# A fused two-layer graph kernel: order of TensorE's steps in the first edge stage, setup loads, scatter turns

## The reference

```python
# x: 100000 x 128 float32; src, dst: 25000 edges, dst sorted
# layer 0: messages of the edges, maximum over the edges of one dst
feat = concatenate([x[dst], x[src] - x[dst]], axis=-1)
messages = relu(feat @ W1 + b1) @ W2 + b2
x = layernorm(x + where(isneginf(segment_max(messages, dst)), 0, segment_max(messages, dst)))
# layer 1: sum over the edges, two products, residual product
h = x + segment_sum(x[src], dst)
h = maximum(h @ V1 + c1, 0) @ V2 + c2
out = layernorm(x + (x @ Wres + bres) + h)
```

## Time and profile before

| What | Value |
|---|---|
| Median of three runs | 1114.36 us |
| The profiled execution, its own time | 1113.68 us |
| Its span in the profile | 1111.9 us |
| PE busy | 1068.9 us (96%) |
| DVE busy | 934.9 us (84%) |
| ACT busy | 896.9 us (81%) |
| GpSimd busy | 765.8 us (69%) |
| Granted TensorE clock, mean | 0.995 |

### The profile page before, as it was taken

How to read it: one execution, slowest core, us unless ns; L and a number is a source line. 1 busy time by engine, 2 the same in 40 slices (tenths; PEclk the granted TensorE clock), 3 DMA queues, 4 the chain that set the end, 5 groups by cost and what they waited for, 6 DMA issues and landing times.

```text
span 1111.9 us, 27074 instructions
## 1 busy us (share of the span) xinstructions
PE 1068.9 (96%) x7463; PEld 835.6 (75%) x7463; DVE 934.9 (84%) x3645; ACT 896.9 (81%) x3888; POOL 765.8 (69%) x798
## 2 busy tenths in 40 slices
PE   5899999999999999999899999999999999999995
PEld 3677877777666666666578888888888878888884
DVE  7799888897888888888868787878787789999993
ACT  2887878787888888888897888888888887777774
POOL 6777777777777777772047777777777777777712
PEclk9999999999999999999999999999999999999998
DMA  5788877875888888877576667676756566666652
GB/s 151 214 244 247 230 244 231 246 233 152 220 222 232 248 232 221 233 223 214 164 232 198 213 191 215 190 214 191 214 166 194 172 202 217 218 217 220 218 171 86
DMA packets 172255, 231.86 MB, mean 209 GB/s; under 512 B 25658, under 2 KB 90791, under 8 KB 172106
## 3 DMA queue, kind: packets, MB, share of 16 engines
q1 hardware_dynamic: 145434, 180.66, 52.0%
q0 software_dynamic: 25088, 48.94, 17.3%
q10 hardware_dynamic: 1584, 0.53, 0.2%
HBM read 129.48 MB, written 102.78 MB: 209 GB/s over the span
## 4 chain that ended last, share of the span: by engine, by line
PE 65%; POOL 19%; issue 8%; DVE 4%; ACT 2%; DMA 1%; SPq 0%; POOLq 0%; DVEq 0%; ACTq 0%
POOL edge_rows L522 17%; PE psY L1125 10%; PE psY L1126 10%; PE psH L1137 10%; PE psE L1118 6%; PE psT L1118 5%; PE psE L1257 4%; PE psE L1126 4%; PE psE L1125 4%; PE psE L1293 4%; PE psE L1248 3%; PE psE L1242 3%; PE psE L1240 3%; POOL xd_early L522 1%; DVE shared L758 1%
## 5 line engine op out<-in xcount | busy, mean ns | idle before, releaser
L1125 PE MATMUL psY<-wc,hT 128*128 128x128 f32 x1568 | 304.1, 276 | 0.5 <-DVE o_rows L646 0.4
L1126 PE MATMUL psY<-wcr,xT 128*128 128x128 f32 x1568 | 303.9, 276 | 0.0
L522 POOL DMA_INDIRECT edge_rows<-x1e_table,idx x196 | 188.8, 963 | 118.5 <-issue 59.4
L526 POOL DMA_INDIRECT out<-edge_rows,idx x196 | 195.0, 995 | 100.0 <-issue 61.9
L1125 PEld LDWEIGHTS psY<-wc,hT 128*128 128x128 f32 x1568 | 240.7, 192 | 13.3 <-issue 13.3
L949 ACT ACTIVATE junk<-psY 128x128 f32<-128x128 f32 x784 | 209.3, 302 | 49.3 <-PE psY L1126 49.1
L1126 PEld LDWEIGHTS psY<-wcr,xT 128*128 128x128 f32 x1568 | 238.8, 193 | 0.0
L522 POOL DMA_INDIRECT edge_rows<-in_x,idx x196 | 189.8, 968 | 65.5 <-issue 59.4
L609 DVE TENSOR_SCALAR x<-x_in,mv,rs 128x128 f32<-128x128 f32 x784 | 221.7, 361 | 0.6
L1137 PE MATMUL psH<-xT,wc 128*128 128x512 f32 x392 | 204.5, 604 | 6.2 <-ACT xT L944 5.5
L1118 PEld LDWEIGHTS psT<-ident,x 128*128 128x128 f32 x784 | 99.2, 143 | 110.1 <-issue 104.1
(11 more groups left out here) (125 smaller groups left out, 1993.4 us busy)
## 6 DMA issues: line engine op xcount, KB each, us to landing
x_in<-in_x SPq DMA_DIRECT2D x196, 256.0 KB
out<-o_rows SPq DMA_DIRECT2D x195, 256.0 KB
src_bc<-src_dram SPq DMA_DIRECT2D x49, 256.0 KB, 4.5
mask<-mask_dram SPq DMA_DIRECT2D x98, 128.0 KB
x1eT_spill<-x1eT SPq DMA_DIRECT2D x49, 256.0 KB, 2.4
x1e_table<-edge_rows SPq DMA_DIRECT2D x49, 256.0 KB, 3.5
x1e_table<-shared SPq DMA_DIRECT2D x49, 256.0 KB, 3.8
x1eT<-x1eT_spill SPq DMA_DIRECT2D x49, 256.0 KB, 3.1
```

The costliest lines, as they stand in the source:

```text
L522: nc.gpsimd.indirect_dma_start(to, None, table, bass.IndirectOffsetOnAxis(idx[:, what, t:t + 1], 0)).then_inc(landed[n % FLIGHT], 16)
L526: nc.gpsimd.indirect_dma_start(table, bass.IndirectOffsetOnAxis(idx[:, SCAT, t:t + 1], 0), frm, None, bounds_check=limit, oob_is_err=False ...
L1125: t_.matmul(to[:, cut(t)], h[:, cut(t)], wc2[:, :], start=t == 0, stop=False, skip_group_check=True)
L1126: last = t_.matmul(to[:, cut(t)], xt[:, cut(t)], wcr[:, :], start=False, stop=t == TILES - 1, skip_group_check=True)
```

## The change

The change has these parts. In stage A, PE's `transposed(n)` moves from h = 1 to h = 0 and `first_product(n-1)` from h = 0 to h = 1; ACT's `copy_xT` and `relu` change places with them. The three whole dense steps that followed steps 49 to 51 are now inside those steps. On DVE, ACT and SP they are still the last thing of the step; on PE they stand ahead of `transpose_x1e`, `center_z` and `transpose_in`. In the setup SP issues x of unit 0 before the source indices, the biases have a semaphore of their own and are issued after the first root, DVE does norm 1 of unit 0 around the index cast, ACT copies the weights instead of DVE, and PE does the first product of unit 0 ahead of the last weight products. In the head `copy_xT` comes ahead of `root`. SP's first two `feed_s` move from behind the head to behind its unit 6. The last scatters get a count for each of the four `stored` semaphores, computed on DVE in `late_stores` when stage B begins.

```diff
@@ walk
             for s in range(GROUPS, STEPS):
-                step_a(s, None, 0)
-                dense(A_LAST + s - GROUPS)
+                step_a(s, A_LAST + s - GROUPS, A_STEPS)
@@ sync
+                if n == HEAD - 2:
+                    sp.wait_ge(s_srcst, 32)
+                    feed_s(0)
+                    feed_s(1)
             def lead_s():
-                sp.wait_ge(s_srcst, 32)
-                feed_s(0)
-                feed_s(1)
+                pass
@@ step_a, sync
                 load_mask(s + 1)
+                if h == A_STEPS:
+                    dense(n)
@@ sync, setup
+            load(0)
             sp.wait_ge(s_iz, 1)
             load_indices(0, src, s_is)
-            load(0)
             load(1)
@@ gpsimd
+            def late_needed(at):
+                return [pool.value_load(late_16[0:1, at, k:k + 1], min_val=0, max_val=16 * BODIES) for k in range(SLOTS)]
+            def await_stores(counts):
                 for k in range(SLOTS):
-                    pool.wait_ge(stored[k], count)
+                    pool.wait_ge(stored[k], counts[k])
                 pool.nop().then_inc(s_turn, 1)
+            pool.wait_ge(s_late, 4)
+            for g in range(LATE, WHOLE):
+                counts = late_needed(g - LATE)
+                pool.wait_ge(res_done, g + 1)
+                await_stores(counts)
+                for t in range(TILES):
+                    scatter_tile(g, t)
             for g in range(WHOLE, GROUPS):
                 pool.wait_ge(res_done, g + 1)
                 for t in range(TILES):
-                    await_stores(count if t < WHOLE_TILES else 16 * BODIES)
-                    if t + 1 < WHOLE_TILES:
-                        count = stores_needed(WHOLE + t + 1)
-                    scatter(out, edge_rows[:, cut(g * TILES + t)], g * TILES + t, scatter_number(g) + t)
+                    await_stores(late_needed(SLOTS + t) if t < WHOLE_TILES else [16 * BODIES] * SLOTS)
+                    scatter_tile(g, t)
@@ vector
+            def late_stores():
+                counts = late_16[:, :, :].rearrange("o n k -> o (n k)")
+                v.tensor_scalar(late_unit[:, :], last_dst[:, LATE:WHOLE + WHOLE_TILES], ROWS.bit_length() - 1, None,
+                                ALU.arith_shift_right).then_inc(s_late, 1)
+                dve.wait_ge(s_late, 1)
+                for k in range(SLOTS):
+                    last = v.tensor_scalar(late_16[:, :, k], late_unit[:, :], SLOTS - k, None, ALU.add)
+                last.then_inc(s_late, 1)
...
             def lead_b():
                 dve.wait_ge(eh_done, GROUPS)
+                late_stores()
@@ vector, setup
+            norm1_stats(0)
+            norm1_var(0)
             dve.wait_ge(s_is, 16 * 4)
             link(v.tensor_copy(idx_f[:, 0, :, :], idx_in[:, 0, :, :]))
-            norm1_stats(0)
-            norm1_var(0)
+            recip(-2)
+            norm1_scale(0)
             dve.wait_ge(s_pe, 1)
             link(v.tensor_copy(idx[:, 0, :], psE[0][:, 0:2 * P]))
@@ scalar
             def head(n):
-                if n == 0:
-                    copy_xT(0)
-                    root(0)
-                else:
-                    dense(n)
+                norm2_var(n - 3)
+                relu(n - 1)
+                copy_xT(n)
+                if n == 0:
+                    keep_weights()
+                root(n)
+                finish(n - 3)
@@ step_a, scalar
-                if n is not None:
+                if h == A_STEPS:
+                    dense(n)
+                elif n is not None:
                     if h == 0:
+                        copy_xT(n)
+                    if h == 1:
                         relu(n - 1)
-                    if h == 1:
-                        copy_xT(n)
@@ scalar, setup
             root(-2)
+            load_biases()
             root(-1)
-            act.wait_ge(s_w, 16 * 11)
+            act.wait_ge(s_b, 16 * 5)
@@ step_a, tensor
                 edge_product2(s - 1)
                 edge_product1(s)
-                if n is not None:
+                if h == A_STEPS:
+                    dense(n)
+                elif n is not None:
                     if h == 0:
+                        transposed(n)
+                    if h == 1:
                         first_product(n - 1)
-                    if h == 1:
-                        transposed(n)
                     if h >= 2:
                         second_half(n - 2, h - 2)
                 transpose_x1e(s - 2)
```

More of the change, by code:

```diff
@@ L554, in _, with stores_needed @@
                     gather(edge_rows[:, cut(g * TILES + t)], x1e_table, PLACE, g * TILES + t, z_number(g) + t)
[L556 to L561, removed]
+            def stores_needed(g):
+                top = g + SLOTS - 1
+                earlier = pool.value_load(stores_16[0:1, top:top + 1], min_val=0, max_val=16 * LAST)
+                return [pool.snap(earlier + 16)] * SLOTS
@@ L570, in _ @@
             pool.wait_ge(s_dv, SETUP_STEPS)
-            count = stores_needed(last_group_of(0))
-            for g in range(WHOLE):
+            counts = stores_needed(0)
+            for g in range(LATE):
                 pool.wait_ge(res_done, g + 1)
-                if g % SLOTS == 0 or g > LATE:
-                    await_stores(count)
+                if g % SLOTS == 0:
+                    await_stores(counts)
                 for t in range(TILES):
-                    if t == TILES - 1 and (g % SLOTS == SLOTS - 1 or g >= LATE):
-                        count = stores_needed(last_group_of(g + 1) if g + 1 < WHOLE else WHOLE)
-                    scatter(out, edge_rows[:, cut(g * TILES + t)], g * TILES + t, scatter_number(g) + t)
+                    if t == TILES - 1 and g % SLOTS == SLOTS - 1 and g + 1 < LATE:
+                        counts = stores_needed(g + 1)
+                    scatter_tile(g, t)
@@ L979, in dense @@
                 norm2_var(n - 3)
+                if n >= UNITS:
+                    root(n)
                 relu(n - 1)
-                root(n)
+                if n < UNITS:
+                    root(n)
                 copy_xT(n)
@@ L1174, in transpose_indices, with last_weights @@
                 last.then_inc(s_pe, 1)
+            def last_weights():
+                t_.matmul(psE[3][:, 0:P], wtmp[:, 1, :], center[:, :], start=True, stop=True)
+                t_.matmul(psE[1][:, 0:P], wtmp[:, 2, :], center[:, :], start=True, stop=True).then_inc(s_pe, 1)
             def head(n):
-                if n > 0:
+                if n == 1:
+                    pe.wait_ge(s_copied, 1)
+                    first_product(0)
+                    last_weights()
+                    transposed(1)
+                elif n > 1:
                     first_half(n)
@@ L1323, in _ @@
             t_.transpose(psE[2][:, 2 * P:3 * P], raw[:, W2R, :], ident[:, :]).then_inc(s_pe, 1)
-            pe.wait_ge(s_dv, SRC_IDX_STEP + 2)
-            t_.matmul(psE[3][:, 0:P], wtmp[:, 1, :], center[:, :], start=True, stop=True)
-            t_.matmul(psE[3][:, P:2 * P], wtmp[:, 2, :], center[:, :], start=True, stop=True).then_inc(s_pe, 1)
             walk(head, dense, lead_s, step_s, lead_a, step_a, lead_b, step_b)
```

61 lines of the change are left out of this document (39 added, 22 removed).

## The result

The changed kernel takes 1118.65 us (median of six runs), the kernel before 1114.58 beside it. The ratio is 1.0036, with a 95% interval of 1.0023 to 1.0049. So it is slower by 4.1 us; 1113.0 was forecast, in a range up to 1115.0. The profiled execution of the changed kernel took 1119.12 us with a span of 1117.3, so the two profiled spans lie 5.4 us apart, 1.3 more than the medians. What follows is read from them.

A forecast was written before the change was run, and what follows sets the result against it. PE, busy for 96% of the span, was taken as the bound, with ACT behind it from step 49. Terms -0.7 + 0 + 3.05 + 0.1 - 3.8 = -1.4 us gave 1113.0 us against the median, range 1110.0 to 1115.0.

The forecast's parts named there:

- First gather: Setup: with x of unit 0 issued earlier, the first gather starts at 8.5 in place of 9.27, 0.8 us early.
- the slower rival: Setup: index loads queue behind x, land at 8 us, first gather 1.9 us late; 1115.7 us in all, 9% chance.
- the chain of gathers runs at its own pace: After the first gather: gathers follow each other some 1.25 us apart, without a stop that matters.
- Stage S: Stage S to A: loads 3.3 us earlier gain PE some 3 us, gathers cap it; net gain 0.7 us.
- the landing moves only with the first gather: Start of stage A: the awaited gather's landing comes earlier only by the first gather's 0.8 us.
- the meeting at group 5: Start of stage A: gather chain and PE's chain arrive practically together at group 5, so a gain in one alone is lost.
- The exchange: Stage A: 0.43 us of PE work moved between intervals gains nothing; bounds 0.5 gained and 0.3 lost over twelve units.
- the 1.4 us of holes in a unit: Stage A: a unit of 23.52 us costs PE 22.15 us of work, the rest being holes, mostly ahead of h = 1 centring.
- The tail: Steps 49 to 51: centring gains 0.92 us, late edge transposes hold ACT, lower clock costs 1.4; loss 3.05 us.
- the 1.65 of the order: Step 50: unit 73 ahead of group 48's edge transposes makes ACT's copy of them start 1.65 us late.
- DVE's counts: Beginning of stage B: seven operations and three waits, about 0.9 us, hidden; cost 0 to 0.3, summed as 0.1.
- The end: Last scatters: finer turns start the last scatter about 0.25 us after the last landing; gain 3.8 us.

The follow-up runs named there:

- e4: The kernel before with only the finer scatter turns of the change: 1111.55 us, ratio 0.9976.
- e12: The kernel before with the source gathers of the last five groups moved behind later destination gathers, nothing else: 1112.60 us, ratio 0.9985.
- e1: The changed kernel with PE's whole dense units of steps 49 to 51 put back behind the edge work: 1114.41 us, ratio 0.9996.
- e3: The changed kernel with the stage A exchange of transposes and first product undone: 1118.36 us, ratio 1.0038.
- e6: The changed kernel with four extra unread products on PE in its wait for unit 72 in step 50: 1116.18 us, ratio 1.0014.
- e2: The changed kernel with the first two loads of source values issued behind the head again: 1115.75 us, ratio 1.0010.
- e5: The changed kernel with five extra unread first products on PE ahead of its wait for the gathers of group 4: 1115.92 us, ratio 1.0010.
- e9: The changed kernel with the last five groups' source gathers moved later and all three dense units behind the edge work on PE: 1106.02 us, ratio 0.9925.
- e10: The changed kernel with the last five groups' source gathers later, all dense units behind PE's edge work, first source loads behind the head: 1107.88 us, ratio 0.9942.

## Why the prediction was wrong

**First gather.** The mechanism was right (8.85, forecast 8.5; the index loads did come later behind x), the term was not. The old setup starts gathering at 9.27, 8.81 (e4) and 9.06 (e12), the new one at 8.57 to 9.10 in eleven executions, so on the mean the new one gains 0.2 us, not 0.8, with ranges that overlap. The index loads landed near 5.9 in place of 4.2, so the slower rival's order was seen, but only 1.7 us late. Moreover the last gather of group 4 was issued at 282.80 to 283.91 in all eight kernels with the old order of gathers, whatever the first one was. The step "the chain of gathers runs at its own pace" failed: most are 1.25 us apart, but 18 to 23 of the first 216 are 1.40 to 1.65, and in the changed kernel's trace five more of these than before outweighed the head start. This is a small part: e1, e3 and e6 issued that gather at 282.8 to 283.2, as before, and were 3.2 to 3.4 us late at step 5 all the same.

**Stage S.** It was right that the gathers cap PE's gain, and that PE would wait for `src_bc`. Three steps failed. PE's gain from the earlier loads was 1.2 us at step 1 (e2), not 3: DVE's wait went, but the rest of that stretch did not follow. The step "the landing moves only with the first gather" failed: an earlier PE brought SP's transfers ahead of the last gather of group 4, and it landed 4.7 us after its issue (283.91 to 288.60), when 3.7 had been enough in the trace of before and 2.5 was in e4. I had set the meeting at group 5 and left out group 4. And the price of the wait was taken as zero. I named the lowered clock for the tail and not here, where the same change made a wait of 5.5 us; e5 gives it as 2.0 to 2.7 us. Gain of 0.7 forecast, 4.1 lost in the profiled executions; against e4, which had PE early and a short wait, the loss at step 5 is 4.7. The 296.79 in that working, for the stalled centring before, is 296.69 in the row; it moves the gain by 0.1.

**The exchange.** Right, in mechanism and size: 23.54 us a unit, a new wait of 0.18 ahead of h = 0, e3 within 0.3 us. Only the 1.4 us of holes in a unit were too many: PE is busy for 22.75 of the 23.52 us from 367.24 to 390.76, and the wait of 0.75 is nearly the whole rest.

**The tail.** Right in mechanism and order: the centring at full clock, ACT's copy 0.9 early, the wait of 3.85 (forecast 3.9), the copy of group 48 late. Mis-sized was the clock: 1.4 us was read from a stretch in which only a part of the work ran at the lower level, while all of unit 73 did, 6.1 us in place of 3.1. e6 has the clock at 2.5 to 3.1 of the 4.2 to 4.9 us. The copy of group 48 was 4.65 us late, which is the 1.65 of the order and 3.0 of the slow unit, and with the clock kept up (e6) the tail is 1.8 us longer than before's. That bears the 1.65 out, though roughly: e6's tail is 0.5 us longer than e1's and 2.7 longer than e9's, with the same order on PE in both as before.

The stretch that the 1.4 us came from does not even repeat. The same waits of about 1.7 and 1.3 us left the centring of step 49 at 2.08, 1.76, 2.08 and 2.03 us in before, e1, e10 and e12, and at 1.16, full clock, in e4 and e9. So the 0.9 us to be gained by that centring were there in some executions only.

**DVE's counts.** No run takes them apart. e4 has them, and its tail is 27.9 us against 27.4 in before and 27.3 in e12, so they cost 0.5 at most by these traces; 0.1 was forecast.

**The end.** 3.8 forecast, 3.0 measured (e4). The reads of counts were not all of the 1.45 us behind the landing; 0.92 remain, where 0.25 was forecast. The 0.4 us of ACT's earlier root were no term of the forecast.

**The sum.** With the measured terms: +4.1 at the start of stage A, 0, +4.2 to 4.9 in the tail, -3.0 to -3.5 at the end, so 5.3 to 5.5, the distance of the two spans; the medians are 4.1 apart. Two terms had the wrong size by the same cause, a clock that falls in a long wait, and one of them, at the start of stage A, the wrong sign by that and by the late landing. The slower rival was another mechanism (indices late), so the 5% for slower did not cover the true one.

What stays open is why some gathers take 0.15 to 0.4 us longer, whether SP's transfers are what held the last gather of group 4 up, and why the kernel before in its profiled execution reached stage A 1.5 to 1.9 us later than e4 and e12, with the same order on PE.

## What to carry to other kernels

An engine that arrives earlier at a transfer which does not come earlier gains nothing, and on TensorE it can lose: its wait grows, the clock falls, and the work behind the wait runs at half speed. It can also release other transfers early, and in these traces the awaited one then landed later; so first move the transfer. Work put into a hole is only a gain if its own inputs are there: in an in-order queue, a unit that waits holds up all behind it, here the few transposes that the bound engine needed. Where a long wait can't be avoided, products that nobody reads keep the clock up (1.5 to 2.7 us each time here), and a meeting of two chains should be read from more than one execution.

## What the runs showed of the hardware

I had not expected that a wait in pieces does it: four waits of 0.4 to 2.4 us with single transposes between them brought the granted clock to 0.50 (288 to 290 us). The low level, 1.2 GHz, lasted over all of a unit of 6.1 us. Nor does one order give one clock: with equal waits on PE the centring of step 49 ran at full clock in two executions and below it in four. The Trainium skill, TensorE: Matmul & The Clock Gate, section What's actually happening, says that the throttled state is the default and activity releases it; e5 and e6, where unread work held the clock at 1.00, agree.

The indirect gathers of one group landed 3.2 to 5.0 us behind their issue in the changed kernel (279.79 to 283.01, and 282.66 to 287.71), and the last of them 2.5 to 5.3 us behind it in seven kernels. With the same order on PE, PE reached step 1 1.9 us apart in two executions (271.14 and 273.02).
